# Row maxima from half of the symmetric score square, by float16 planes and DMA transposes; Exp over 1024 columns; PV of a key block in one go

## The reference

```
xn = (x - mean) / sqrt(var + 1e-5)
attention(xn):   z = layernorm(xn) * g + b
                 q, v = z @ w_q.T + b_q, z @ w_v.T + b_v;   k = q
                 per image and head (16 heads of 16):
                 scores = q @ q.T / 4;  attn = softmax(scores);  o = attn @ v
                 out = concat(o) @ w_out.T + b_out
ffn(xn):         gelu(xn @ ternary(W1).T + b1) @ ternary(W2).T + b2
result = x + attention(xn) + ffn(xn)
```

## Time and profile before

| | us |
|---|---|
| median of three runs | 1458.41 |
| the three runs | 1463.61, 1457.3, 1458.41 |
| profiled execution, span | 1462.7 |

### The profile page before, as it was taken

One profiled execution on the slowest core, in us unless ns is written; L12 is line 12 of the kernel. 1 busy time (PEld: TensorE's weight loads), 2 busy tenths in 40 slices (PEclk: granted clock), 3 DMA queues, 4 the chain that ended last, 5 costly groups with the idle time before them and its releaser, 6 DMA issues.

```text
span 1462.7 us, 31753 instructions
## 1 busy us (share of the span) xinstructions
PE 1396.9 (96%) x13166; PEld 445.3 (30%) x13166; DVE 1351.0 (92%) x1430; ACT 1243.2 (85%) x2284; POOL 113.7 (8%) x246
## 2 busy tenths in 40 slices
PE   6899988999999999999999999999999999999999
PEld 4666542222222222222222222222222222222244
DVE  7767789999999999999999999999999999999944
ACT  5564543999999999999999999899999999999975
POOL 2000006000000000000000000000111100001100
PEclk8999998999999999999999999999999999999999
DMA  5012000000000000000000001001212100011122
GB/s 228 15 40 69 30 15 1 28 30 29 29 30 29 30 30 29 26 26 29 29 30 29 30 29 34 30 31 34 59 59 59 59 30 32 31 32 59 38 92 86
DMA packets 28529, 60.65 MB, mean 41 GB/s; under 512 B 6200, under 2 KB 11736, under 8 KB 28130
## 3 DMA queue, kind: packets, MB, share of 16 engines
q1 hardware_dynamic: 27810, 56.99, 11.5%
q10 hardware_dynamic: 576, 1.65, 0.3%
HBM read 41.29 MB, written 16.77 MB: 40 GB/s over the span
## 4 chain that ended last, share of the span: by engine, by line
DVE 54%; PE 37%; ACT 5%; issue 3%; DMA 2%; POOL 0%; SPq 0%; ACTq 0%; DVEq 0%
DVE part_max L838 50%; PE ps L367 13%; PE ps L384 8%; PE ps L330 5%; PE ps L1067 3%; ACT w L1046 3%; PE ps L1136 2%; PE ps L1082 2%; DVE w L830 1%; PE ps L458 1%; ACT w L1017 1%; DMA rows<-in_rows 1%; PE ps L439 1%; PE ps L1108 1%; ACT hidden L1012 1%
## 5 line engine op out<-in xcount | busy, mean ns | idle before, releaser
L838 DVE TENSOR_REDUCE part_max<-ps 128x1 f32<-128x1024 f32 x1024 | 1171.5, 1216 | 16.8 <-PE ps L330 13.8
L1046 ACT ACTIVATE w<-ps 128x512 f32<-128x512 f32 x2048 | 1104.5, 596 | 86.5 <-PE ps L384 50.6
L367 PE MATMUL ps<-w,v_ones 128*32 128x256 f32 (+1 forms) x7440 | 623.8, 407 | 0.4
L384 PE MATMUL ps<-qry,key 50*128 50x512 f16 x1984 | 424.1, 389 | 21.2 <-ACT w L1046 20.7
L330 PE MATMUL ps<-qry,key 48*128 48x512 f16 x2048 | 412.6, 381 | 15.1 <-DVE part_max L838 11.7
L367 PEld LDWEIGHTS ps<-w,v_ones 128*32 128x32 f32 x7440 | 146.6, 108 | 371.1 <-issue 206.8
L384 PEld LDWEIGHTS ps<-qry,key 50*128 50x128 f16 x1984 | 103.9, 93 | 475.3 <-ACT w L1046 443.2
L330 PEld LDWEIGHTS ps<-qry,key 48*128 48x128 f16 x2048 | 102.2, 95 | 46.1 <-DVE part_max L838 33.1
L637 POOL COPY v_ones<-v_all 128x128 f32<-128x128 f32 x64 | 18.6, 291 | 805.8 <-PE ps L367 805.8
L1067 PE MATMUL ps<-w_ternary,w 128*128 128x256 f16 x512 | 62.1, 278 | 6.2 <-DVE w L830 6.2
L1008 ACT ACTIVATE q_split<-ps,sigma_bq 128x512 f16<-128x512 f32 x16 | 11.0, 687 | 66.2 <-PE ps L1082 66.2
(11 more groups left out here) (144 smaller groups left out, 462.4 us busy)
## 6 DMA issues: line engine op xcount, KB each, us to landing
key<-q_parts SPq DMA_DIRECT2D x64, 128.0 KB
qry<-q_parts SPq DMA_DIRECT2D x64, 128.0 KB
o_heads<-o_evacuated SPq DMA_DIRECT2D x31, 256.0 KB, 10.2
resid<-in_x SPq DMA_DIRECT2D x8, 512.0 KB, 13.9
q_parts<-q_split SPq DMA_DIRECT2D x16, 256.0 KB, 2.5
key<-q_parts SPq DMA_DIRECT2D x64, 64.0 KB
qry<-q_parts SPq DMA_DIRECT2D x64, 64.0 KB
out<-resid SPq DMA_DIRECT2D x7, 512.0 KB, 3.6
```

The lines of the kernel that those rows point to most:

```text
L367: mm = eng.matmul(pv[32 * c:32 * c + 2 * D, c0:c1], vst[:, kb, :], prob[kb % 2][:, c * BANK + c0:c * BANK + c1], start=(kb == 0), stop=(kb ...
L384: eng.matmul(ring_bank(v, i, False), key[v][r:r + KROWS, kb * P:(kb + 1) * P], qry[v][r:r + KROWS, c * BANK:(c + 1) * BANK], start=True, s ...
L838: dve.tensor_reduce(part_max[:, a // 2, a % 2:a % 2 + 1], pa[a % 2], AX.X, ALU.max).then_inc(s_r, 1)
L1046: act.activation(prob[kb % 2][:, c * BANK:(c + 1) * BANK], ring_bank(k, i, last), ACT.Exp, scale=exp_scale).then_inc(s_e, 1)
```

## The change

- **Pass A from half the square.** For key block i only the eight column blocks i to i + 7 (mod 16) are made, and for the eight blocks of `WIDE` a ninth, i + 8: 1024 or 1152 columns in one tile of three banks (`pr`). `row_pass` on DVE scales them by 1/SHIFT, writes them as float16 into `planes` in SBUF and takes the row's maximum by its accumulator, in one instruction. The row block of another key block needs the same scores by column: plane b of key block i belongs to key block i + b. `columns_step` takes the elementwise maximum of the planes b of this key block with the planes b + 1 of the one before, so that at the end one plane per column block holds the maximum over its keys, still by partition.
- **DMA transposes.** `columns_over`, on SP's queue, transposes these 16 blocks of 128 x 128 float16 in three DMAs (4, 4 and 8 blocks) into `col_t`; `halve` and `fold` on DVE reduce along the free axis from 128 to one and join the result with the row maxima.
- **Exp over 1024 columns.** B's products come in pairs into two pairs of banks; ACT takes 32 Exps of 1024 columns per head in place of 64 of 512.
- **PV in one go**: `pv_step`, four matmuls of 512 queries per block.
- **Order.** Per block: B pair, a row step 10 blocks ahead, B pair, the maximum's transpose at block 13, PV of the block before. Before the first head the ten row steps run by themselves.
- **Banks and memory.** `py` has one bank in place of two. 14 tiles of setup move into one arena, over which `planes` lie later.

The core of the diff:

```diff
-AHEAD = 2
-STEPS = 4
+AHEAD = 10
+MAX_AT = 13
+FOLD_AT = 5
+WIDE = (0, 1, 2, 3, 4, 5, 6, 15)
-PERIOD = "BBAPBBAPBBAPBBAP"
...
+        arena = sb("score_arena", [P, (SPAN + 1) * PLANE], F16)
+        planes = arena[:, :].rearrange("p (b s n) -> p b s n", b=SPAN + 1, s=NBLK)
...
-        pb = [bank(4), bank(5), bank(7)]
-        pv = bank(6)
-        py = [bank(2), bank(3)]
+        pr = bank(0, 3)
+        pb = [bank(3, 2), bank(5, 2)]
+        pv = bank(7)
+        py = bank(1)
...
+        def row_step(eng, a, v, i):
+            n = NBLK * (a - 1) + i
+            eng.wait_ge(s_r, NA + n)
+            if i == WIDE[-1]:
+                eng.wait_ge(s_mc, a)
...
+            for _, j, o, c, size in pieces:
+                r = tile(j)
+                mm = eng.matmul(pr[:, o:o + size], key[v][r:r + ROWS, i * P:(i + 1) * P],
+                                qry[v][r:r + ROWS, c:c + size], start=True, stop=True)
+            mm.then_inc(s_a, 1)
...
+        def pv_step(eng, h, kb):
+            eng.wait_ge(s_e, NE * h + 2 * (kb + 1))
...
             for c in range(NCH):
+                mm = eng.matmul(pv[32 * c:32 * c + 2 * D, :], vst[:, kb, :],
+                                prob[kb % 2][:, c * BANK:(c + 1) * BANK], start=(kb == 0), stop=(kb == NBLK - 1))
...
+        def b_pair(eng, h, v, kb, x):
+            e = NE * h + 2 * kb + x
+            if kb == 0 and x == 0:
                 eng.wait_ge(s_mr, 32 * (h + 1))
+            wait(eng, s_e, e - 1)
...
+        def pe_head(eng, h):
+            v = h % ROT
+            for kb in range(NBLK):
+                b_pair(eng, h, v, kb, 0)
+                ahead_step(eng, NBLK * h + kb + AHEAD)
+                b_pair(eng, h, v, kb, 1)
+                if kb == MAX_AT:
+                    max_transpose(eng, h + 1)
+                if kb:
+                    pv_step(eng, h, kb - 1)
+                elif h:
+                    pv_step(eng, h - 1, NBLK - 1)
...
-                wait(eng, s_yd, n - 1)
+                wait(eng, s_yd, n)
...
+            def columns_over(a, n):
+                j0, j1 = ((SPAN, SPAN + NCH), (SPAN + NCH, NBLK), (0, SPAN))[n]
+                s0 = (j0 + SPAN * (a % 2)) % NBLK
+                sp.wait_ge(s_cw, NBLK * (a - 1) + (SPAN + NCH - 2, NBLK - 2, NBLK)[n])
+                if n == 0:
+                    wait(sp, s_ft, 4 * (a - 1))
+                sp.dma_start_transpose(col_t[:, j0:j1, :], planes[:, 1, s0:s0 + j1 - j0, :].rearrange("p s n -> p (s n)")).then_inc(s_ct[n], 16)
...
                     load_head(h + 2, (h + 2) % ROT)
+                if h + 1 < NH:
+                    columns_over(h + 1, 0)
                 store_o(h - 1)
                 if h + 1 < NH:
+                    columns_over(h + 1, 1)
+                    columns_over(h + 1, 2)
                     max_rows_in(h + 1, (h + 1) % ROT)
...
+            def row_pass(a, i):
+                n, w = NBLK * (a - 1) + i, width(i)
+                dve.wait_ge(s_a, NA + n + 1)
...
+                if a > 1 and i in (0, NCH - 1, SPAN - 1):
+                    dve.wait_ge(s_ct[(0, NCH - 1, SPAN - 1).index(i)], 16 * (a - 1))
+                dve.tensor_scalar(planes[:, 0:w, slot(a, i), :], pr[:, 0:w * P].rearrange("p (b n) -> p b n", n=P),
+                                  1.0 / SHIFT, None, ALU.mult, ALU.max, accum_out=row_max[:, a % 2, i:i + 1]).then_inc(s_r, 1)
+
+            def columns_step(a, i):
+                b, n = width(i - 1) - 1, NBLK * (a - 1) + i
+                dve.wait_ge(s_r, NA + n + 1)
+                wait(dve, s_cw, n - 1 if i > 1 else 0)
+                own = planes[:, 1:b, slot(a, i), :]
+                dve.tensor_tensor(own, own, planes[:, 2:b + 1, slot(a, i - 1), :], ALU.max).then_inc(s_cw, 1)
...
+            def halve(a, n, size):
+                wait(dve, s_ft, 4 * (a - 1) + n)
+                dve.tensor_tensor(col_t[:, :, 0:size], col_t[:, :, 0:size], col_t[:, :, size:2 * size], ALU.max).then_inc(s_ft, 1)
+
+            def fold(a):
+                halve(a, 1, P // 4)
+                halve(a, 2, P // 8)
+                dve.wait_ge(s_ft, 4 * (a - 1) + 3)
+                dve.tensor_reduce(col_max[:, :], col_t[:, :, 0:P // 8], AX.X, ALU.max, negate=True).then_inc(s_ft, 1)
...
+                dve.scalar_tensor_tensor(out=neg_max[:, :], in0=row_max[:, a % 2, :], scalar=-1.0, in1=col_max[:, :],
+                                         op0=ALU.mult, op1=ALU.min).then_inc(s_m, 1)
+
+            def between(a, i):
+                if i == 0 and a > 1:
+                    columns_step(a - 1, NBLK - 1)
+                if i == 1 and a > 1:
+                    columns_round(a - 1)
+                if i == FOLD_AT and a > 1:
+                    for n in range(3):
+                        dve.wait_ge(s_ct[n], 16 * (a - 1))
+                    halve(a - 1, 0, P // 2)
+                if i > 1:
+                    columns_step(a, i - 1)
+                if i == FOLD_AT and a > 1:
+                    fold(a - 1)
...
+            for a in range(1, NH):
+                for i in range(NBLK):
+                    row_pass(a, i)
+                    between(a, i)
...
+                        act.activation(prob[kb % 2][:, x * W:(x + 1) * W], pb[x], ACT.Exp, scale=exp_scale).then_inc(s_e, 1)
```

More of the change, by code:

```diff
@@ L353, in pv_half @@
[L353 to L365, removed]
-            for c in range(NCH):
[L367 to L370, removed]
@@ L387, in pe_head @@
[L387 to L413, removed]
@@ new lines, in b_pair @@
+        def b_pair(eng, h, v, kb, x):
+            e = NE * h + 2 * kb + x
+            if kb == 0 and x == 0:
+                eng.wait_ge(s_mr, 32 * (h + 1))
+            wait(eng, s_e, e - 1)
+            for j in range(2):
+                c = 2 * x + j
+                r = tile(c)
+                mm = eng.matmul(pb[x][:, j * BANK:(j + 1) * BANK], key[v][r:r + KROWS, kb * P:(kb + 1) * P],
+                                qry[v][r:r + KROWS, c * BANK:(c + 1) * BANK], start=True, stop=True)
+            mm.then_inc(s_b, 1)
@@ L417, in last_at, with last_pair @@
         def last_at(n):
             return [m for m in range(NBLK) if min(m // TG * TG + TG + 1 + m % TG, NBLK) == n]
-        def last_chunk(eng, i):
+        def last_pair(eng, n, x):
             h, v = NH - 1, (NH - 1) % ROT
-            kb, c = i % NBLK, i // NBLK
-            if i == 0:
+            if n == 0 and x == 0:
                 eng.wait_ge(s_mr, 32 * (h + 1))
[L426 to L429, removed]
+            eng.wait_ge(s_e, NE * h + 2 * n + x - 1)
+            for j in range(2):
+                i = NCH * n + 2 * x + j
+                kb, c = i % NBLK, i // NBLK
+                r = tile(i)
+                mm = eng.matmul(pb[x][:, j * BANK:(j + 1) * BANK], key[v][r:r + KROWS, kb * P:(kb + 1) * P],
+                                qry[v][r:r + KROWS, c * BANK:(c + 1) * BANK], start=True, stop=True)
+            mm.then_inc(s_b, 1)
@@ new lines, in columns_step, with columns_round @@
+            def columns_step(a, i):
[4 more added lines that the diff above has]
+                dve.tensor_tensor(own, own, planes[:, 2:b + 1, slot(a, i - 1), :], ALU.max).then_inc(s_cw, 1)
+            def columns_round(a):
+                b, i = width(NBLK - 1) - 1, NBLK - 1
+                dve.wait_ge(s_cw, NBLK * a - 1)
+                j0 = slot(a, 0)
+                own = planes[:, 1, j0:j0 + b - 1, :]
+                dve.tensor_tensor(own, own, planes[:, 2:b + 1, slot(a, i), :], ALU.max).then_inc(s_cw, 1)
@@ L862, in _ @@
             results(0)
-            steps = iter([(0, a) for a in range(NA)] + [(1, a) for a in range(2)])
+            steps = iter(range(NA))
             def first_rows(n):
                 for _ in range(n):
-                    max_step(*next(steps))
+                    max_step(0, next(steps))
             for g in range(1, NG - 1):
@@ L1164, in _ @@
             group(0)
-            steps = iter([(0, a) for a in range(NA)] + [(1, a) for a in range(2)])
+            steps = iter(range(NA))
             def first_a():
-                h, a = next(steps, (None, None))
-                if h is None:
+                a = next(steps, None)
+                if a is None:
                     return
                 if a == 0:
-                    pe.wait_ge(s_ld[h], 128)
-                a_step(pe, h, h, a)
+                    pe.wait_ge(s_ld[0], 128)
+                a_step(pe, 0, 0, a)
             def first_a_early(calls=iter(range(TG * KF // 4))):
```

216 lines of the change are left out of this document (121 added, 95 removed).

## The result

The changed kernel takes 1434.5 us (median of four runs, 1433.0 to 1436.8) against 1459.2 (median of four) for the kernel before: the ratio is 0.982 (0.980 to 0.984), 25 us or 1.8% faster. The forecast was 1364 us, 95 us faster: the sign holds, the size is off by a factor of nearly four. The time lies above the 1320 to 1425 us of the forecast proper and within its outer ends, 1319 and 1440; it is almost the number of rival B, 1433, for reasons that were only in part B's.

The account below looks back on a forecast made before the run. Taken as tight: DVE and PE, 37.3 us per head. First evacuation 294.4, 29 x 33.7 = 977.3, last head 31.8, tail 64.5: 1368.0, less 4.3 gives 1364 us; range 1320 to 1425 (0.66), outer ends 1319 and 1440.

Parts of the forecast that it names:

- rival B: Dearer handoffs per head: accumulator at 0.19 us, Exp at its upper end, stalls of 2 us; 1433 us, chance 0.13.
- two things come due at once: At block 6, the load of head h+2 and the next head's first transpose: 0.7 us per head, bounds 0 and 2.
- the fold: Once per head on DVE, halvings and a last reduction take 1.95 us, other engines waiting: +1.8 us per head.
- Rival D: Column steps on DVE at one element per cycle, 0.94 us each, 38.7 us per head: 1517 us, slower; chance 0.06.
- double rate: DVE's column step on float16 in SBUF takes half of 1.05 ns per element: 0.50 us between starts.
- The accumulator: Writing the row maximum in DVE's row pass adds 0.10 us, between nothing and 0.186.
- the Exp of 1024 columns: On ACT, 1.03 us each, or 0.95 apart: 1.90 us per block, from 2.06.
- Rival C: Third transpose lands later than 7.8 us, so DVE stands at the fold: 1436 to 1610 us; chance 0.11.
- B's first pair: Before the first head, ten row steps that can't overlap put B's first chunk at 253.7 us: +13.2 us.
- One bank for the projection: At the end, each project waits for add_y, 0.5 or 0.2 us: 5 us in all, ends 0 and 8.

Follow-up runs that it names:

- load16: Changed kernel with four DMAs of each head's load cut in two, 12 DMAs in place of 8, same bytes: 1375.3 us, 0.9415 of the kernel before.
- l16_spread: load16 with the fold's operations spread behind the column steps of blocks 3, 4 and 5: 1341.7 us, 0.9189 of the kernel before.
- no_loads: Changed kernel without the loads of heads 3 to 31, all heads using the first three loads: 1373.6 us in one run.

## Why the prediction was wrong

| part of the span | forecast | measured |
|---|---|---|
| to the first evacuation | 294.4 | 288.4 |
| first to last evacuation | 1009.1 | 1075.6 |
| behind the last evacuation | 64.5 | 67.2 |
| span | 1368.0 | 1431.2 |

**What failed, first: "two things come due at once ... bounds 0 and 2 us; I take 0.7".** The coincidence was seen and the place named, and the size was wrong. Between the first and the last evacuation load16 takes 1308.2 - 290.1 = 1018.1 us, 57.5 less than the changed kernel: 1.9 us per head in place of 0.7. In the 25 intervals without a pair it is 0.9, close to the term, and in the five pair heads 6.9, far outside its bounds. I had set the lateness of the load against one engine's need and taken the difference of two near numbers, 13.6 and 13.5 us. It is a chain: the load late, the first transpose behind it, the row pass behind that. And the pair heads (40 to 43 us) were never looked at, though the trace of before has their DMAs. I read 0.08 of DMA share in the earlier trace rows as the end of a load without asking why a transfer of 768 KB keeps two engines busy for ten microseconds.

**Second, a term that was missing: the granted clock inside a head.** I charged the fold 1.8 us as DVE time and said that PE, B, PV and ACT would wait with it. They did: 1.78 us of idle PE in load16. What I left out is what the idle does to the clock: in load16 it costs it in 20 of 25 usual heads, 1.4 us each. In the changed kernel ten usual heads and all pair heads run at a lower clock, there also behind the waits for load and transpose (as in the head at 611 us above). I had seen a low clock at the start of the heads, 0.66 in the earlier trace rows, and used it only there. Spreading the fold gave back 33.7 us of load16's run.

**What held.** Per head, 33.64 forecast (the mean of the 30) + 1.2 (the queue, 1.9 for 0.7) + 1.2 (clock and the fold in one piece, (1018.1 - 982.8) / 30 between load16 and l16_spread) - 0.2 (all the rest, by difference) = 35.84, against 35.85. Most heads of l16_spread take 32.3 us, where my sum without the 0.7 was 33.0; its pair heads, longer, bring the mean to (1272.7 - 289.9) / 30 = 32.8. Rival D is out: the column step over 768 float16 elements takes 0.55 us undisturbed and over 896 0.62, so some 0.5 ns per element, not 1.05 (the group's mean at 768, 0.577, has in it the steps that Pool slows). This agrees with the Trainium skill ("VectorE: DVE Perf Modes", section "The perf-mode tier table"), whose double rate the forecast took. Rival B, whose 1433 us is nearly the time measured, is right in one of its three terms: the stalls came, 1.9 us per head for its 2. The accumulator took 0.083 us and not 0.19, and the Exp of 1024 columns 1.028 us as forecast. The clock, for which it had no term, made up the rest, so its number is partly luck. Rival C is half right: a transpose did come late, yet not the third and not by its own price. With no load before it in the queue it lands in 2.4 us (no_loads, median); the 23 us in SP's queue did not occur, SP needs 1.2 us to issue one.

**The parts of the change.** PV in one go gave nothing measurable in load16, in one run; it was not tried with the clock kept, where alone the Exps' gain showed. Exp over 1024 columns gave nothing while the clock fell, and 21 us once it did not. The half square must carry the rest, by difference, since no run undoes it: 32 reductions 1.13 us apart were 36.2 us of DVE per head, and in l16_spread a whole head takes 32.3.

**The ends.** B's first pair came at 249.4 us in place of 253.7, since the ten row steps take 1.9 to 2.3 us each from an earlier start. One bank for the projection shows as forecast; PE waits 0.61 us in a block for `add_y`:

```profile
1365.60 0.81 PE L483 MATMUL ps<-wo_parts,hidden 128*128 128x256 f16 x6 [0.61 <-DVE resid L1021]
```

## What to carry to other kernels

When a change shortens the lead of a load, look at what the load does on the DMA engines and not only at when it ends: a source whose outer dimension is 2 ran on two engines of sixteen, free of cost while nothing waited on it or on what stood behind it. Here its lateness was passed on to the transposes behind it in the same queue; an earlier issue and one more buffer didn't cure it, a shorter occupation did. Look at the unusual turns of a loop by themselves: five pair heads of 30 held 34.5 of the 57.5 us. And where several engines run within a few per cent of each other under one fixed order, put a burst of one engine's work into pieces: here the burst cost its length, and then the clock.

## What the runs showed that was not expected

A column step on DVE takes 0.62 us, and over 1.0 us while Pool adds the bias in SBUF beside it, in some of the blocks. In load16's timeline Pool's additions, then one step beside them and one behind:

```profile
231.35 25.28 POOL L671 TENSOR_TENSOR resid<-resid,bias_row 128x256 f32<-128x256 f32 x32
...
244.22 1.13 DVE L908 TENSOR_TENSOR score_arena<-score_arena 128x896 f16<-128x896 f16 x1
...
256.70 0.56 DVE L908 TENSOR_TENSOR score_arena<-score_arena 128x768 f16<-128x768 f16 x1
```

The DVE operation and its operands are of the same kind in both (896 and 768 elements); the difference of 0.57 us is not their size, since 128 elements more cost 0.07 us undisturbed. And SP's issue of a transpose takes 1.2 us as a rule and 5.1 to 6.0 us in four pair heads of the changed kernel, right behind the loads of pair and head, time in which the queue issues nothing else; with the short load the longest takes 1.97.
